# Graph layer with scatter-add and layernorm on one core: blocks and edge rounds taken in a circle from block 25

## The reference

```
x: (100000, 64) f32; src, dst: (50000,) i32; edge_attr: (50000, 32) f32
dst = min(int(100000 * uniform ** 2), 99999), then both src, dst sorted by dst

msg = concat(x[src], edge_attr) @ W1 + b1          # 128 hidden
agg = segment_sum(msg, dst, 100000)
y   = x + concat(x, agg) @ W2 + b2                 # 64 columns
out = (y - mean(y)) / sqrt(var(y) + 1e-5)          # per row
```

## Time and profile before

| | |
|---|---|
| median of 3 runs | 714.42 us (713.59 to 715.35) |
| the profiled execution, its own time | 712.24 us |
| its span, first to last instruction | 710.3 us |
| mean granted TensorE clock | 0.907 of full |
| busy: PE / PEld / DVE / ACT / POOL | 566.6 / 507.2 / 519.7 / 397.4 / 398.9 us |

### The profile page before, as it was taken

The page is one execution under the profiler, slowest core; times in us unless marked ns, Lnnn a source line. Parts: engine busy times, 40 slices in busy tenths (PEclk is TensorE's granted clock), DMA queues, the critical chain, the costliest instruction groups (busy, mean ns, idle before and its releaser), DMA issues. The chain is left out here.

```text
span 710.3 us, 28935 instructions
## 1 busy us (share of the span) xinstructions
PE 566.6 (80%) x8370; PEld 507.2 (71%) x8371; DVE 519.7 (73%) x1820; ACT 397.4 (56%) x2012; POOL 398.9 (56%) x418
## 2 busy tenths in 40 slices
PE   1365798998888888898889888898888888873774
PEld 1355687888777877787778878787777777763653
DVE  2684677778788877778778778778888888863443
ACT  0011478777777777777777777776544445532101
POOL 5777657777757777766774777765744444000000
PEclk9955799999999999999999999999999999985555
DMA  2122345545545555545555545554433333220002
GB/s 63 33 38 38 81 123 147 136 120 132 147 117 149 127 124 138 141 122 126 142 136 136 133 120 131 139 132 114 99 83 81 81 81 96 81 59 7 2 1 60
DMA packets 168746, 71.33 MB, mean 100 GB/s; under 512 B 61570, under 2 KB 162447, under 8 KB 168720
## 3 DMA queue, kind: packets, MB, share of 16 engines
q1 hardware_dynamic: 104592, 51.74, 25.5%
q0 software_dynamic: 12544, 12.87, 9.8%
q10 hardware_dynamic: 51584, 6.41, 5.8%
HBM read 45.37 MB, written 25.60 MB: 100 GB/s over the span
## 5 line engine op out<-in xcount | busy, mean ns | idle before, releaser
L381 POOL DMA_INDIRECT feat<-in_x,src_idx x392 | 391.9, 1000 | 197.9 <-issue 117.7
L806 DVE TENSOR_SCALAR onehot<-node_of_col,group_base,dst_of 128x256 bf16<-128x256 bf16 x944 | 288.0, 349 | 90.8 <-issue 81.2
L490 PEld LDWEIGHTS ps_y<-z_window,onehot 128*128 128x128 bf16 x5664 | 195.1, 100 | 48.8 <-DVE z_window L809 30.2
L490 PE MATMUL ps_y<-z_window,onehot 128*128 128x64 bf16 x5664 | 213.5, 196 | 18.0 <-DVE z_window L809 14.1
L596 ACT ACTIVATE square<-ps_y 128x64 bf16<-128x64 f32 x784 | 162.1, 238 | 94.7 <-PE ps_y L481 91.9
L596 ACT ACTIVATION_READ_ACCUMULATOR square<-ps_y 128x1 f32 x784 | 159.1, 224 | 0.0
L417 PE MATMUL ps_z<-wz,feat_t 97*128 97x64 f32 x784 | 106.0, 293 | 31.5 <-DVE z_rest L725 31.4
L481 PE MATMUL ps_y<-wx,x_t 128*128 128x128 f32 x784 | 114.9, 291 | 18.5 <-ACT x_t L589 12.7
L417 PEld LDWEIGHTS ps_z<-wz,feat_t 97*128 97x128 f32 x784 | 100.3, 207 | 40.3 <-DVE z_rest L725 36.5
L809 DVE COPY z_window<-z 128x384 bf16 x472 | 121.6, 258 | 0.0
L481 PEld LDWEIGHTS ps_y<-wx,x_t 128*128 128x128 f32 x784 | 99.1, 197 | 22.3 <-ACT x_t L589 16.5
(11 more groups left out here) (113 smaller groups left out, 214.3 us busy)
## 6 DMA issues: line engine op xcount, KB each, us to landing
xin<-in_x SPq DMA_DIRECT2D x97, 256.0 KB
out<-yout SPq DMA_DIRECT2D x97, 256.0 KB
feat<-in_x,src_idx POOLq DMA_INDIRECT x392
feat<-in_edge_attr ACTq DMA_DIRECT2D x96, 64.0 KB
z<-in_src SPq DMA_DIRECT2D x1, 192.0 KB
z<-in_dst SPq DMA_DIRECT2D x1, 192.0 KB
xin<-in_x SPq DMA_DIRECT2D x1, 128.0 KB
out<-yout SPq DMA_DIRECT2D x1, 128.0 KB
```

The source lines that it names most:

```text
L381: nc.gpsimd.indirect_dma_start(out=feat[h][:, feat_at(k) + feat_slot(c), 0:C], out_offset=None, in_=x[:, :], in_offset=bass.IndirectOffset ...
L490: mm = nc.tensor.matmul(ps_y[h][:, col:col + C], onehot[h][:, g, s, a, :], z_window[h][:, g, s, part * C:(part + 1) * C], start=False, sto ...
L806: ins = nc.vector.tensor_scalar(onehot[h][:, g, s, :, :], node_of_col[:, :, :], base, dst_of[:, bass.ds(firsts[g] + (at + s), 1)], ALU.add ...
```

## The change

The order is turned round and cut open in the middle. Chunks, batches and blocks are taken upwards, but start at block 25 and at edge round 24 (chunk 192), go up to the last, and continue from 0: blocks 25 to 97 and 0 to 24, edge rounds 24 to 48 and 0 to 23. A round's number `k` still counts from 0 in the order of work, and `chunk_at` turns it into a place in `z`. The index tables are copied straight (two copies in place of four). The last batch is three whole chunks that end at the last edge; the edges that it shares with the batch before have no `dst` in one of the two. The table's formula (`need`) counts a block's last chunk round the circle, with about a dozen small DVE operations more. A hardware loop can't wrap round, so ACT's loop becomes a loop (rounds 4 to 22), four written-out rounds (23 to 26) and a loop (27 to 47), and DVE's becomes a loop (4 to 26), round 27 written out, and a loop (28 to 49). SP's loop of loads and stores is split at unit 36, which now holds the partial block 97 together with block 0. `AHEAD` and `LAG` stay as they are.

```diff
-LAST_CHUNK = -(-E // P) - 1
+BATCH_EDGES = CB * P
+LAST_EDGES = E - (CB - 1) * P
+TWICE = (BATCHES - 1) * BATCH_EDGES - LAST_EDGES
...
 AHEAD = 2.125
+FIRST_BLOCK = 25
+FIRST_ROUND = 24
+FIRST_CHUNK = 2 * CB * FIRST_ROUND
+CUT_UNIT = (BLOCKS - 1 - FIRST_BLOCK) // 2
+TURN = PAIRS - FIRST_ROUND
...
+        def chunk_at(k, turned=False):
+            if isinstance(k, int):
+                return 2 * CB * ((k + FIRST_ROUND) % PAIRS)
+            return 2 * CB * k + (FIRST_CHUNK - (CHUNKS if turned else 0))
...
+            sp.wait_ge(x_used[0], CUT_UNIT)
+            whole, cut = tail_parts(x)
+            sp.dma_start(xin[0][0:TAIL_PARTS, TAIL_GROUPS, :], cut).then_inc(x_cut_loaded, 16)
+            load_x(CUT_UNIT, 1, x_blocks[0])
+            sp.wait_ge(x_cut_loaded, 16)
+            sp.dma_start(xin[0][:, 0:TAIL_GROUPS, :], whole).then_inc(x_loaded[0], 16)
...
-            nc.gpsimd.memset(xin[0][:, :, :], 0.0).then_inc(s_clear, 1)
...
-                    col = (2 * k + h) * CB + c
+                    col = chunk_at(k) + CB * h + c
...
-            with act.Fori(LAG + 2, PAIRS - 2) as k:
-                edge_round(k)
-                z_mids(k - 2)
+            def act_round(k, turned=False):
+                edge_round(k, turned)
+                z_mids(k - 2, turned)
                 for_units(act, mybir.EngineType.Activation, k - LAG, unit)
...
+            with act.Fori(LAG + 2, TURN - 2) as k:
+                act_round(k)
+            for k in range(TURN - 2, TURN + 2):
+                act_round(k)
+            with act.Fori(TURN + 2, PAIRS - 1) as k:
+                act_round(k, turned=True)
...
-            nc.vector.tensor_copy(src_idx[:, 0:LAST_CHUNK + 1], ps_t[0][:, LAST_CHUNK::-1])
-            nc.vector.tensor_copy(src_idx[:, LAST_CHUNK + 1:CHUNKS], ps_t[0][:, LAST_CHUNK + 1:CHUNKS])
-            nc.vector.tensor_copy(dst_of[:, 0:LAST_CHUNK + 1], ps_t[1][:, LAST_CHUNK::-1])
-            nc.vector.tensor_copy(dst_of[:, LAST_CHUNK + 1:CHUNKS], ps_t[1][:, LAST_CHUNK + 1:CHUNKS]).then_inc(s_idx, 1)
-            dve.wait_ge(s_idx, 1)
+            nc.vector.tensor_copy(dst_of[:, :], ps_t[1][:, 0:CHUNKS]).then_inc(s_dve, 1)
+            nc.vector.tensor_copy(src_idx[:, :], ps_t[0][:, 0:CHUNKS]).then_inc(s_idx, 1)
...
+            link(nc.vector.tensor_scalar(last[:, :], last[:, :], -1.0, None, ALU.add))
             link(nc.vector.tensor_scalar(need[:, :], first[:, :], 3.0, None, ALU.add))
             link(nc.vector.tensor_tensor(need[:, :], need[:, :], last[:, :], ALU.max))
+            link(nc.vector.tensor_scalar(far_first[:, :], first[:, :], float(FIRST_CHUNK), float(CHUNKS - 1), ALU.is_lt, ALU.mult))
+            link(nc.vector.scalar_tensor_tensor(out=far_first[:, :], in0=need[:, :], scalar=float(FIRST_CHUNK),
+                                                in1=far_first[:, :], op0=ALU.is_ge, op1=ALU.mult))
+            link(nc.vector.tensor_scalar(wrapped[:, :], need[:, :], float(FIRST_CHUNK), float(CHUNKS), ALU.is_lt, ALU.mult))
+            link(nc.vector.scalar_tensor_tensor(out=need[:, :], in0=need[:, :], scalar=float(-FIRST_CHUNK),
+                                                in1=wrapped[:, :], op0=ALU.add, op1=ALU.add))
+            link(nc.vector.tensor_tensor(need[:, :], need[:, :], far_first[:, :], ALU.max))
...
-            with dve.Fori(LAG + 2, PAIRS + 1) as k:
+            with dve.Fori(LAG + 2, TURN + 2) as k:
                 dve_round(k)
+            dve_round(TURN + 2)
+            with dve.Fori(TURN + 3, PAIRS + 1) as k:
+                dve_round(k, turned=True)
             dve_round(PAIRS + 1)
```

More of the change, by code:

```diff
@@ L44 @@
 AHEAD = 2.125
+FIRST_BLOCK = 25
[3 more added lines that the diff above has]
+TURN = PAIRS - FIRST_ROUND
 FAR = float(1 << 20)
 EPS = 1e-5
-assert BATCHES == BLOCKS == 2 * PAIRS and LAST_CHUNK < CHUNKS - 1 and BLOCKS <= P
+assert BATCHES == BLOCKS == 2 * PAIRS and 0 <= TWICE < P and BLOCKS <= P
+assert (BLOCKS - 1 - FIRST_BLOCK) % 2 == 0
 def gnn_residual_layernorm(nc, x, src, dst, edge_attr, W1, b1, W2, b2, out, scratch):
@@ L108, in gnn_residual_layernorm @@
         round_no = sb("round_no", [PAIRS, 1])
+        wrapped = sb("wrapped", [P, G])
         units_row = sb("units_row", [1, PAIRS + 1], i32)
@@ L273, in _ @@
                 sp.dma_start(b2c[32 * r:32 * r + 1, :], b2.rearrange("(o f) -> o f", o=1)).then_inc(s_wload, 16)
-            sp.wait_ge(x_cut_loaded, 16)
-            sp.dma_start(xin[0][:, 0:TAIL_GROUPS, :], whole).then_inc(x_loaded[0], 16)
-            sp.dma_start(xin[1][:, :, :], x_block(1)).then_inc(x_loaded[1], 16)
+            for h in range(2):
+                sp.dma_start(xin[h][:, :, :], x_blocks[FIRST_BLOCK + h]).then_inc(x_loaded[h], 16)
             sp.wait_ge(s_steps, 2)
@@ L301, in store, with store_round, load_round @@
                 sp.dma_start(dst_ap, yout[h][:, :, :].rearrange("p (g a) c -> p g (a c)", g=G)).then_inc(out_stored[h], 16)
-            def store_round(k, top=None):
-                top = BLOCKS - 1 - 2 * k if top is None else top
+            def store_round(k, at, cut=0):
                 for h in range(2):
-                    free_yout(k, h)
+                    free_yout(k, h, cut)
                 for h in range(2):
-                    store(k, h, out_full[top - h])
+                    store(k, h, out_blocks[2 * k + at + h])
             for h in range(2):
                 sp.sem_inc(yout_free[h])
-            for h in range(2):
-                load_x(1, h, x_block(2 + h))
-            for h in range(2):
-                load_x(2, h, x_block(4 + h))
-            for h in range(2):
-                free_yout(0, h)
-            sp.wait_ge(out_ready[0], 2)
+            def load_round(k, at):
+                for h in range(2):
+                    load_x(k, h, x_blocks[2 * k + at + h])
+            low, high = FIRST_BLOCK, FIRST_BLOCK - BLOCKS
+            load_round(1, low)
+            load_round(2, low)
+            store_round(0, low)
+            with sp.Fori(2, CUT_UNIT - 1) as k:
+                load_round(k + 1, low)
+                store_round(k - 1, low)
+            sp.wait_ge(x_used[0], CUT_UNIT)
[4 more added lines that the diff above has]
+            sp.dma_start(xin[0][:, 0:TAIL_GROUPS, :], whole).then_inc(x_loaded[0], 16)
+            store_round(CUT_UNIT - 2, low)
+            load_round(CUT_UNIT + 1, high)
+            store_round(CUT_UNIT - 1, low)
+            load_round(CUT_UNIT + 2, high)
+            for h in range(2):
+                free_yout(CUT_UNIT, h)
+            sp.wait_ge(out_ready[0], CUT_UNIT + 2)
             whole, cut = tail_parts(out)
@@ L322, in _ @@
             sp.dma_start(cut, yt[0:TAIL_PARTS, TAIL_GROUPS, :]).then_inc(out_stored[0], 16)
-            store(0, 1, out_block(1))
-            with sp.Fori(2, PAIRS - 1) as k:
-                top = sp.snap(BLOCKS - 2 * k)
-                for h in range(2):
-                    load_x(k + 1, h, x_full[top - (3 + h)])
-                store_round(k - 1, top + 1)
-            store_round(PAIRS - 2)
-            store_round(PAIRS - 1)
+            store(CUT_UNIT, 1, out_blocks[0])
+            with sp.Fori(CUT_UNIT + 2, PAIRS - 1) as k:
+                load_round(k + 1, high)
+                store_round(k - 1, high, cut=1)
+            store_round(PAIRS - 2, high, cut=1)
+            store_round(PAIRS - 1, high, cut=1)
             sp.wait_ge(out_stored[0], 16 * (PAIRS + 1))
@@ L621, in _ @@
                 act.sem_inc(squared[h])
-            act.wait_ge(s_clear, 8)
-            load_ea_first()
-            load_ea(0, 1)
-            act.wait_ge(s_const, 13)
+            act.wait_ge(s_clear, 7)
+            for h in range(2):
+                load_ea(0, h)
+            act.wait_ge(s_const, 14)
             nc.scalar.activation(std_eps[:, :], eps[:, :], ACT.Sqrt)
@@ L755, in _ @@
             link(nc.vector.tensor_tensor(extra[:, :], last[:, :], first[:, :], ALU.subtract))
-            link(nc.vector.tensor_scalar(extra[:, :], extra[:, :], -1.0, 0.0, ALU.add, ALU.max))
+            link(nc.vector.tensor_scalar(extra[:, :], extra[:, :], 0.0, None, ALU.max))
             link(nc.vector.tensor_copy(steps[:, G + 2:STEP], extra[:, :]))
```

125 lines of the change are left out of this document (57 added, 68 removed).

## The result

| | before | changed |
|---|---|---|
| median of 4 runs each, side by side | 714.0 us (713.09 to 715.35) | 734.62 us (731.32 to 736.22) |
| the profiled execution / its span | 712.24 / 710.3 us | 731.32 / 729.4 us |
| mean granted TensorE clock | 0.907 | 0.93 |

The ratio is 1.0281 with an interval of 1.024 to 1.0322: slower by some 20 us. The forecast was 734.6 us. The two profiled executions differ by 19.1 us, and the two are compared in what follows.

The account below looks back on a forecast made before the run. PE and DVE were taken as near their limit through round 36, DVE as the bound from round 41. Late start 7.2, code copies 3 and round 37 onward 10.0 add 20.2 us to the median 714.42: 734.6 us, range 716 to 752.

Parts of the forecast that it names:

- start of round 37: End of the light rounds: near 464 us where it was 454.3, from 7.2 for the late start and 3 for code copies.
- rounds 37, 38, 39: Rounds with the moved heavy blocks and the one behind: 39.5, 29.1 and 17.8 us, third pairs at half clock.
- rounds 40 to 47: Second-pair rounds at 16.6 us each, with rounds 40, 42 and 45 empty at 6.5 each.
- from 667.6: round 49, units 45 to 48, drain, copies: End of the kernel: 6.5 for the empty round, 42.8 behind the edges, 7.2 drain, 4 for code copies.
- The start: Rounds 4 and 5: unit 0 begins at 80.6, 9.5 us later; cost 7.2 us, between 4 and 9.5.
- Copies of code in mid-run: DVE entering two new copies in rounds 27 and 28, ACT five: cost 3 us, between 0 and 9.5.
- Heavy blocks: Blocks 0 to 2, now in rounds 37 and 38: third pairs stay at half clock, 1.49 us each as in the tail.
- The third rival: Rounds 37 and 38: TensorE's clock holds at 2.4 GHz, a third pair takes 0.97 us; 708.9 us, chance 0.10.
- Empty rounds: Rounds 40, 42, 45, 49: DVE waits for ACT, 5.5 us, plus 1.0 for the clock; 6.5 each, 26.0 together.
- The tail: Behind the edges: unit 45 13.3, unit 46 8.5 + 2.5, units 47 and 48 17.0; drain 7.2, copies 4 us.
- The first rival: New code copies, mid-run and end: all idle at each entry comes again, uncovered; 751.4 us, chance 0.17.
- the second (723.6): Rival on copies and empty rounds: copies cost nothing, an empty round leaves the clock alone; 723.6 us, chance 0.15.

## Why the prediction came out right

The time is right (734.6 forecast, 734.62 measured), but that it fits so closely is luck: four of its terms are off and cancel. Even the last 1.1 us of the span do: the median lies 3.3 us above the profiled execution, where the prediction took 2.2. By its own steps:

| term | forecast | measured | error |
|---|---|---|---|
| start of round 37 | 464.5 | 460.1 | -4.4 |
| rounds 37, 38, 39 | 39.5 + 29.1 + 17.8 | 38.4 + 28.3 + 15.4 | -4.3 |
| rounds 40 to 47 | 3 x 6.5 + 5 x 16.6 = 102.5 | 108.9 | +6.4 |
| round 48 | 16.6 | 16.5 | -0.1 |
| from 667.6: round 49, units 45 to 48, drain, copies | 6.5 + 42.8 + 7.2 + 4 = 60.5 | 61.8 | +1.3 |
| span | 730.5 | 729.4 | -1.1 |

- **The start.** The first unit came at 80.83, as worked out. The step that failed is what follows from it: the prediction carried the 7.2 us over unchanged, but some is caught up. At the start of round 6 the new kernel has run one unit where the old one had run three, so it is 94.24 + 17.0 - 102.15 = 9.1 us late; round 7's two units take 16.1 us in place of 19.3 and round 11's 18.2, which gives 4.3 back. That leaves 4.8 of the 5.8 at round 37. The kernel before with an empty round 4 agrees, with 5.3 at round 6, checks included.
- **Copies of code in mid-run.** Priced at 3 (0 to 9.5). The other 1.0 us at round 37 is all that is left for the copies and everything else, and rounds 27 and 28 show nothing on their own. So it was nearer the lower end. The Trainium skill's rule in "Runtime: NRT & Kernel Launch", section "Instruction fetch mechanics", that a branch out of the fetched window stalls, would give the upper end by itself. The trace agrees with it at the start and at the end (PE's 2.66 us at the first unit, 3.23 at unit 45, DVE's 2.97 at unit 46) and shows no lost time in the light rounds. That these gaps are fetches is argued from their places, not shown.
- **Heavy blocks.** The mechanism was right to 0.01 us a pair: 1.49. The third rival (the clock holds) falls by that row and by the clock of 0.71 in round 37. All three rounds were over-priced, 37 and 38 by 1.1 and 0.8 us, round 39 by 2.4: the clock was back at 0.97, so the 1.2 us added for it weren't due, and the round is cheaper than 16.6 besides.
- **Empty rounds: the term that was mis-sized.** An empty round and the one behind it take 25.7, 25.2 and 25.7 us; less 16.6 that is 8.9 for an empty round where 6.5 was priced (bounds 2.3 to 9.4). The wait was priced well: from DVE's last `yout` (ends at 542.12) to its next one-hots (550.75) pass 8.6 us, where 3.0 pass between rounds 46 and 47 before, so 5.6 more, and 5.5 were forecast. The step that was mis-sized is the clock, put at 1.0 and worth about 3.3: behind the gap `message` (3.68 for 2.00 us) and the transposes of `xin` (1.91 for 1.04) run at half clock, 2.6 us slower together, and DVE waits 3.15 us for PE before its fifth one-hots, where round 44 shows no wait. The load of the edge attributes, which the prediction left out, is not part of it, by the chain in the trace and by what its early issue changed. Why PE's clock falls there but not in every such pause no run shows.
- **The tail.** Units 47 and 48 took 16.7 us (17.0 priced) and the drain 7.2. Unit 45 took 16.2 where 13.3 was priced (its first transposes at half clock, 1.73 us for seven, and DVE 1.64 us on "issue" between its blocks) and unit 46 14.2 where 11.0 was (DVE's 2.97, PE's 1.08). Without copies the sum from 667.6 was 56.5; if the rest of it holds, they cost about 5.3, not 4. Round 48's entry cost nothing, as its second pairs have slack on PE.
- **The clock at the end.** The profiled execution of the changed kernel has a mean clock of 0.93 against 0.907 and is slower: the better clock in the tail bought nothing, since the heavy blocks, which had it low before, take the low clock along (0.71 and 0.80 in rounds 37 and 38). The mean itself says little: the other three executions of the changed kernel had 0.882 to 0.892.

The first rival (copies dear, 751.4 us) falls by rounds 27 and 28 and by the 5.3 us at the end where it had 14.3, the second (723.6) by the 8.9 us of an empty round.

## What to carry to other kernels

Moving the heaviest work from the tail into the middle didn't make it cheaper here, where every engine runs in program order: its gaps and its low clock came along, at 1.49 us a pair in both places. What moves the time is how the order fits the pace. Count from the schedule's table the rounds in which a queue has nothing to do, before and after; here each cost 5 to 7 us over its own work, and with the pace and the cut retuned all 20 us came back. When an empty slot is priced, follow every wait to the one that ends last: a load that lost its cover looked costly here and cost nothing, while the low clock behind the idle time cost three times what was put down for it.

## What the runs showed of the hardware

- Range checks at run time on two loaded numbers cost 0.3 us in a light round (rounds 15 to 29: 11.15 us each against 10.86), up to 0.4 later on. A counter in a register cost at most 0.04 us a round.
- Taking away PE's wait of 1.50 us for a load left the matmuls behind it where they were (7.89 us after the round's start in both) and at half clock (3.68 and 3.67 us): PE waited 1.87 us for DVE instead.
- The same program took 723.77 us and 1079.04 us on the same chip in different series, with 269.4 us of PE's idle time on "issue" ahead of the one-hot matmuls in the slow one and 0.3 in the other. Ratios from such a series (0.9998 to 1.0075) hide a difference that is 1.5 to 2.8% otherwise.
- Entering two unused copies of some 200 instructions in mid-run cost DVE nothing that shows (rounds of 10.3 and 11.4 us), while at the end, where it enters its last copy, it stood 2.97 us on "issue".
